# An attention block with fused feed-forward: loads for the last stage two blocks sooner, and another interleaving of eight steps on TensorE

## Chip, cores and metric

One core of a Trainium2 chip. The metric is the device time of one execution in microseconds. Three runs of the kernel before gave 2847.31, 2848.78 and 2850.04 us.

## The reference

Two residual layers on `x` of shape (4, 2048, 256), all in fp32, 16 heads of 16 channels:

```python
x = x + attention(layernorm(x), Wq, bq, Wk, bk, Wv, bv, Wo, bo)   # logits = q k^T * 4, softmax over 2048 keys
y = layernorm(x)
y_prev = y shifted by one token (zero ahead of the first)
xr, xk = mu_r * y + (1 - mu_r) * y_prev, mu_k * y + (1 - mu_k) * y_prev
out = x + sigmoid(xr @ W_r) * (square(relu(xk @ W_k)) @ W_v)
```

The softmax subtracts each query's largest logit, so for each query and head the maximum over all 2048 keys has to be known before its exponentials.

## The kernel before, in words

Two stages lie in one program: `stage_attend` (layer norm, projections, attention) and `stage_mix` (output projection, second norm, feed-forward). Constants and buffers of the second stage live in `MixInputs`, called `ahead` in the first, because parts of it start early.

**Attention.** Work is cut into 64 blocks (`ITS`), each of 512 queries for four heads; a block has 16 steps (`CH`), each of 128 keys. For a step:
- Two fills (`scores`, L1130 ff.) put logits into PSUM, each for two heads: two f16 matmuls (L1136) side by side on two halves of the rows of the array, 512 columns each. PSUM has two pairs of banks for them, so `fill(n)` waits until ACT is through with fill n - 2 (`s_exp`).
- ACT takes the exponential of each pair of banks (L921, 128x1024) into one of three `p_sb` buffers (in the profile `m_gate`, `m_y` and `p_x`).
- `times_v` (L1217 ff., matmul at L1233) multiplies by V with a column of ones: four column groups of the array, fp32. It runs whole (512 columns) or in two halves (256 columns each, `times_v(n, 0)` and `times_v(n, 1)`); in the first step of a block the first half is always whole and the second does nothing. It waits for both exponentials of its step.

**The maxima** of a later block are found meanwhile. A pack (`peaks`, L1172 ff., matmul at L1192) makes the logits of 128 queries of two heads against 512 keys in two of three banks, again two f16 matmuls; the pack waits until the first bank of the pack before has been reduced (`s_mx`). DVE reduces each bank to a column of `mx` (L998). Some packs are "larger": ahead of them two key ranges are subtracted (`differences`, L1151, a fill of its own that ACT copies through a ReLU into `copied`, L930), and DVE adds and reduces in one custom operation with an accumulator read (L993), so that one pack stands for two. `LARGER` says which packs of a period these are, `COPY_AT` at which fills the copies stand, `EXPS_BEFORE` before which exps ACT runs them.

**Order.** Eight steps are a period (`SPAN`), two periods a block. In a period PE runs 16 fills for exps, 2 fills for copies, 14 packs and 8 `times_v`, in an order written out by hand in `tensor` (L1348 to L1397). Maxima run three periods (`LEAD`) ahead of the fills; the loop has 125 periods, and the rest follows with `last_fills`, into which `early` mixes parts of the second stage. In every second period `turn` (L1195 ff.) transposes the block's maxima; its place among the fills is `TURN_AT`. They come from `of_block` on DVE (L977) and `chain` on POOL (L803 ff.); ACT copies the result to `a_mrows` (L897), and SP sends it into the rows of the next block's queries (`rows`, L699), for which the first fill of that block waits (`s_mr`). Because all engines follow written orders, the unit numbers of fills, copies and turns come from the constants at the head (L488 to L506).

**The way into the last stage.** SP runs `body(it)` per block and ahead of some bodies, at L768 to L790, loads for the second stage. They hang together: `load_sums` brings the denominators of a sequence, DVE inverts them (`invert`, L1109), `store_inverse` writes them out (SP waits for it), `load_heads` brings numerators and inverses, and POOL multiplies them (`heads`, L858, in the trace L317) for the output projection, which `early` starts on PE. In the kernel before POOL runs `heads` of blocks 0 and 1 ahead of the last `chain`.

Of the kernel before, what the change touches and what calls it, by code (L numbers as in the profile page):

```python
# [32 lines left out]
ITS = UNITS * QB  # L33
# [440 lines left out]
def stage_attend(ctx, nc, psum, x, wqT, wkT, wvT, bq, bk, q_d, k_d, kd_d, v_d, sums_d, inputs, ahead):  # L474
# [16 lines left out]
    FULL, LESS = 16, 14  # L491
    LARGER = (4, 7)
    COPY_AT = (0, 11)
    EXPS_BEFORE = (0, 10)
    COPIES = 2 * (PERIODS - LEAD)
# [6 lines left out]
    CHAIN = 5  # L502
    FILLS_AHEAD = 3
    TURN_AT = 14
    FIRST_LEAD = QB + 2
# [165 lines left out]
    def sync(sp):  # L671
# [95 lines left out]
        for it in range(ITS):  # L767
            if it == ITS - 4:  # L768
                ahead.load_constants(sp)
                for seq in range(B - 1):  # L770
                    ahead.load_sums(sp, seq)
            if it == ITS - 2:
                ahead.store_inverse(sp, 0)
                sp.wait_ge(ahead.s_rden[0], DMA)
                for n in range(2):
                    ahead.load_heads(sp, n)
                for n in range(2):
                    ahead.load_x(sp, n)
                for n in range(2, 4):
                    ahead.load_heads(sp, n)  # L780
# [12 lines left out]
    def gpsimd(pool):  # L793
# [61 lines left out]
        for pit in range(1, ITS):  # L855
            if pit % QB == 0:
                copy_v(pit // QB, range(CH // 2))
            if pit == ITS - 1:  # L858
                for n in range(2):
                    ahead.heads(pool, n)  # L860
            chain(pit)
            if pit % QB == 0:
                copy_v(pit // QB, range(CH // 2, CH))
# [108 lines left out]
    def vector(dve):  # L972
# [132 lines left out]
        for n in range(FULL * LEAD, PACKS):  # L1105
            if n == first_pack(PERIODS - 2):
                ahead.spread_bias(dve)
# [22 lines left out]
    def tensor(te):  # L1130
# [195 lines left out]
        for blk in range(BLOCKS):  # L1326
# [15 lines left out]
            lead(blk, 4)  # L1342
        av.wait(te, BLOCKS - 1, "v1")
        for n in range(3):
            fill(n)
        for n in range(0):
            peaks(FULL * LEAD + n)
        for p in range(PERIODS - LEAD):  # L1348
            f, n, c = FILLS * p, FULL * LEAD + LESS * p, SPAN * p
            fill(f + 3)  # L1350
            fill(f + 4)
            peaks(n)
            times_v(c)
            peaks(n + 1)
            fill(f + 5)
            times_v(c + 1, 0)
            peaks(n + 2)
            fill(f + 6)
            fill(f + 7)
            times_v(c + 1, 1)  # L1360
            peaks(n + 3)
            fill(f + 8)
            times_v(c + 2, 0)
            peaks(n + 4)
            fill(f + 9)
            times_v(c + 2, 1)
            fill(f + 10)
            peaks(n + 5)
            times_v(c + 3, 0)
            fill(f + 11)  # L1370
            peaks(n + 6)
            fill(f + 12)
            times_v(c + 3, 1)
            fill(f + 13)
            peaks(n + 7)
            times_v(c + 4)
            peaks(n + 8)
            if p % 2 and p + 1 < PERIODS:
                turn((p + 1) // 2)
            fill(f + 14)  # L1380
            times_v(c + 5, 0)
            peaks(n + 9)
            fill(f + 15)
            times_v(c + 5, 1)
            fill(f + 16)
            peaks(n + 10)
            fill(f + 17)
            times_v(c + 6, 0)
            peaks(n + 11)
            fill(f + 18)  # L1390
            times_v(c + 6, 1)
            fill(f + 19)
            peaks(n + 12)
            times_v(c + 7, 0)
            fill(f + 20)
            peaks(n + 13)
            times_v(c + 7, 1)  # L1397
        for n in range(SPAN * (PERIODS - LEAD), STEPS):
# [298 lines left out]
```

## Time and profile before

| | us |
|---|---|
| profiled execution | 2846.68 |
| its span, first to last instruction | 2844.8 |
| PE busy (modelled ends) | 2783.0 |
| DVE busy | 2528.2 |
| ACT busy | 2516.7 |
| POOL busy | 377.9 |

The projections take the first 230 us, the attention loop runs from there to about 2540, and the last stage ends the program. In a timeline a row is a start, a length, an engine, a line, an operation with its tiles and a count; `x8` of L1233 is one visit of `times_v`. Records of consecutive operations may overlap, so the distance of starts says more than the length.

### The profile page before, as it was taken

Reading aid. Unit: us, or ns where it says so; the run is one execution under the profiler, and the core shown is the slowest. Engines: PE = TensorE matmul, PEld = TensorE weight load, DVE = VectorE, ACT = ScalarE, POOL = GpSimd, SP = SyncE. Lnnn points to the kernel's source line nnn. Section 1 sums busy time; section 2 is a strip of 40 time slices with the busy share of each in tenths; the row PEclk is TensorE's granted clock in tenths of the full one; section 3 lists DMA queues with packets and bytes.
Section 4 is the critical chain, followed back from the end, with each engine's and each line's share of the span. In section 5 each row is a group of like instructions: output and inputs, shape, how many; then the busy total and the mean of one; then the engine's idle time right before and its main releaser. Section 6 shows DMA issues by size and latency. Waiting matters only on the chain.

```text
span 2844.8 us, 60963 instructions
## 1 busy us (share of the span) xinstructions
PE 2783.0 (98%) x24132; PEld 907.4 (32%) x24132; DVE 2528.2 (89%) x4794; ACT 2516.7 (88%) x2874; POOL 377.9 (13%) x752
## 2 busy tenths in 40 slices
PE   8999999999999999999999999999999999999998
PEld 4543222222222222222222222222222222224776
DVE  4567999999999999999999999999999999975773
ACT  6768999999999999999999999999999999986555
POOL 6762000000000000000000000000000000013541
PEclk9999999999999999999999999999999999999999
DMA  5642000000000000000010101010101000123431
GB/s 172 198 152 74 18 20 20 22 22 22 22 22 22 22 22 22 22 17 26 11 31 8 32 11 32 11 33 11 33 11 32 11 28 15 31 79 98 161 108 45
DMA packets 135276, 124.41 MB, mean 44 GB/s; under 512 B 49872, under 2 KB 117328, under 8 KB 134992
## 3 DMA queue, kind: packets, MB, share of 16 engines
q1 hardware_dynamic: 134992, 120.52, 13.7%
q8 instruction: 191, 3.13, 0.4%
q14 instruction: 93, 0.76, 0.1%
HBM read 72.75 MB, written 47.19 MB: 42 GB/s over the span
## 4 chain that ended last, share of the span: by engine, by line
PE 73%; ACT 16%; issue 5%; DVE 4%; DMA 1%; SPq 0%; POOLq 0%; POOL 0%; ACTq 0%; DVEq 0%
PE psum L1233 30%; PE psum L1136 16%; PE psum L1192 14%; ACT m_gate L921 4%; ACT p_x L921 4%; ACT m_y L921 4%; PE psum L1256 3%; PE psum L1569 2%; PE psum L443 2%; PE psum L1151 2%; PE psum L1267 1%; ACT a_copied L930 1%; PE psum L1590 1%; DVE m_split L413 1%; DMA a_qs<-a_mrows 1%
## 5 line engine op out<-in xcount | busy, mean ns | idle before, releaser
L998 DVE TENSOR_REDUCE a_mx<-psum 128x1 f32<-128x512 f32 x3096 | 1958.3, 684 | 134.3 <-PE psum L1192 92.5
L1136 PE MATMUL psum<-a_qs,a_ks 50*128 50x512 f16 x4096 | 774.6, 385 | 12.2 <-DMA a_qs<-a_mrows 7.5
L921 ACT ACTIVATE m_gate<-psum 128x1024 f32<-128x1024 f32 x684 | 674.9, 1029 | 44.7 <-PE psum L1136 39.3
L921 ACT ACTIVATE p_x<-psum 128x1024 f32<-128x1024 f32 x682 | 673.0, 1029 | 41.1 <-PE psum L1136 35.6
L921 ACT ACTIVATE m_y<-psum 128x1024 f32<-128x1024 f32 x682 | 673.0, 1029 | 36.9 <-PE psum L1136 31.3
L1192 PE MATMUL psum<-a_ks,a_qs 48*128 48x512 f16 x3596 | 696.5, 384 | 4.5 <-DVE a_mx L998 4.1
L1233 PE MATMUL psum<-m_gate,a_vst 128*32 128x256 f32 (+1 forms) x4736 | 418.4, 425 | 4.0 <-ACT m_gate L921 0.9
L1233 PE MATMUL psum<-p_x,a_vst 128*32 128x256 f32 (+1 forms) x4728 | 417.6, 425 | 3.1
L1233 PE MATMUL psum<-m_y,a_vst 128*32 128x256 f32 (+1 forms) x4728 | 417.3, 425 | 3.0
L1136 PEld LDWEIGHTS psum<-a_qs,a_ks 50*128 50x128 f16 x4096 | 197.6, 93 | 546.4 <-issue 140.5
L1192 PEld LDWEIGHTS psum<-a_ks,a_qs 48*128 48x128 f16 x3596 | 175.1, 93 | 556.2 <-DVE a_mx L998 435.6
L993 DVE CUSTOM_DVE_ANT_0 a_copied<-psum,a_copied 128x512 f32<-128x512 f32 x500 | 325.0, 688 | 18.3 <-PE psum L1192 1.9
L930 ACT ACTIVATE a_copied<-psum 128x1024 f32<-128x1024 f32 x250 | 256.8, 1027 | 0.5 <-PE psum L1151 0.5
L807 POOL MEMSET a_mx<- 128x8 f32 x64 | 7.2, 113 | 1455.8 <-DVE a_m L977 1455.8
L1233 PEld LDWEIGHTS psum<-m_gate,a_vst 128*32 128x32 f32 x4736 | 93.7, 108 | 201.6 <-issue 164.7
L1233 PEld LDWEIGHTS psum<-p_x,a_vst 128*32 128x32 f32 x4728 | 93.7, 108 | 200.3 <-issue 165.8
L1233 PEld LDWEIGHTS psum<-m_y,a_vst 128*32 128x32 f32 x4728 | 93.7, 108 | 199.8 <-issue 166.5
L800 POOL COPY a_vst<-a_vin 128x64 f32<-128x64 f32 x256 | 60.1, 238 | 694.9 <-PE psum L1233 694.9
L1151 PE MATMUL psum<-a_kd,a_qs 48*128 48x512 f16 x500 | 96.2, 381 | 0.4 <-ACT m_v L886 0.4
L822 POOL TENSOR_TENSOR m_split<-m_whole,m_split 128x512 f16<-128x512 f32 x64 | 73.7, 1157 | 72.1 <-ACT m_split L909 71.8
L907 ACT ACTIVATE m_whole<-psum,p_sb,p_gain 128x512 f32<-128x512 f32 x64 | 49.5, 773 | 27.7 <-PE psum L1256 27.7
L363 DVE TENSOR_TENSOR m_whole<-psum,m_x 128x512 f32<-128x512 f32 x24 | 16.4, 689 | 58.8 <-PE psum L443 51.2
(120 smaller groups left out, 1641.5 us busy)
## 6 DMA issues: line engine op xcount, KB each, us to landing
m_x<-x SPq DMA_DIRECT2D x24, 512.0 KB, 5.1
a_qs<-q_parts SPq DMA_DIRECT2D x384, 32.0 KB, 2.1
sums<-a_o SPq DMA_DIRECT2D x256, 34.0 KB
q_parts<-m_split SPq DMA_DIRECT2D x16, 512.0 KB, 3.2
v_rows<-m_v SPq DMA_DIRECT2D x16, 512.0 KB, 2.7
k_parts<-m_split SPq DMA_DIRECT2D x16, 512.0 KB, 3.9
a_ks<-k_parts SPq DMA_DIRECT2D x64, 128.0 KB
a_vin<-v_rows SPq DMA_DIRECT2D x64, 128.0 KB, 5.5
```

The source lines that it names most:

```text
L443: mm = te.matmul(bank[:, (t % 2) * C:(t % 2 + 1) * C], self.hT[blk % 2][:, k, t * P:(t + 1) * P], self.w_sb["o"][:, k, :], start=(k == 0), ...
L800: pool.tensor_copy(v_st[:, c, :, 0:D], v_in[:, u % 2, c, :].rearrange("p (g d) -> p g d", g=G)).then_inc(s_vc, 1)
L822: least.done(pool.tensor_tensor(parts[s][:, j, 1, :], full[s][:, j, :], parts[s][:, j, 0, :], ALU.subtract))
L921: ac.activation(p_sb[n % WEIGHTS][:, 2 * pair:2 * pair + 2, :], psum[:, at:at + 2, :], ACT.Exp, scale=SCALE).then_inc(s_exp, 1)
L930: ac.activation(copied[:, :, :], psum[:, at:at + 2, :], ACT.Relu).then_inc(s_exp, 1)
L993: dve.tensor_tensor_reduce(out=copied[:, par, :], in0=psum[:, bank(at), :], in1=copied[:, par, :], scale=1.0, scalar=LEAST, op0=ALU.add, o ...
L998: dve.tensor_reduce(peak, psum[:, bank(at), :], AX.X, ALU.max).then_inc(s_mx, 1)
L1136: mm = te.matmul(psum[:, pair_of_banks(u) + par, :], ks[row:row + MR, (it // QB) % 2, pair, c * P:(c + 1) * P], qs[row:row + MR, it % QRIN ...
L1151: mm = te.matmul(psum[:, pair_of_banks(u) + par, :], qs[row:row + SR, pit % QRING, at:at + P], kd[row:row + SR, (pit // QB) % 2, pair, :], ...
L1192: te.matmul(psum[:, bank(slot(n, par)), :], qs[row:row + SR, pit % QRING, at:at + P], keys, start=True, stop=True).then_inc(s_sp, 1)
L1233: mm = te.matmul(psum[32 * g:32 * g + 32, O, at:at + width], v_st[:, c, g, :], p_sb[n % WEIGHTS][:, g, at:at + width], start=(c == 0), sto ...
L1256: mm = te.matmul(psum[:, j % 2, :], w_sb[n][:, k, h * P:(h + 1) * P], xnT[blk % 2][:, k, :], start=(k == 0), stop=(k == KH - 1))
```

## The change

Steps move and constants change; no operation is added or left out.
- `FILLS_AHEAD` 3 to 4: four fills stand ahead of the loop instead of three, and three packs as well (before: none), so the loop body runs `fill(f + 4)` to `fill(f + 21)` and `peaks(n + 3)` to `peaks(n + 16)`.
- Copies at fills 1 and 13 instead of 0 and 11, larger packs 3 and 13 instead of 4 and 7.
- The turn at fill 7 instead of 14.
- Whole `times_v` for steps c + 1 and c + 7; before, c and c + 4.
- SP, POOL and DVE: loads and their partners two blocks (DVE: four periods) sooner; `heads` behind `chain` of block 61 instead of ahead of that of block 63.

```diff
-    LARGER = (4, 7)
-    COPY_AT = (0, 11)
-    EXPS_BEFORE = (0, 10)
+    LARGER = (3, 13)
+    COPY_AT = (1, 13)
+    EXPS_BEFORE = (1, 12)
-    FILLS_AHEAD = 3
-    TURN_AT = 14
+    FILLS_AHEAD = 4
+    TURN_AT = 7
@@ sync
-            if it == ITS - 4:
+            if it == ITS - 6:
                 ahead.load_constants(sp)
                 for seq in range(B - 1):
                     ahead.load_sums(sp, seq)
-            if it == ITS - 2:
+            if it == ITS - 4:
                 ahead.store_inverse(sp, 0)
                 sp.wait_ge(ahead.s_rden[0], DMA)
                 for n in range(2):
                     ahead.load_heads(sp, n)
                 for n in range(2):
                     ahead.load_x(sp, n)
+            if it == ITS - 3:
                 for n in range(2, 4):
                     ahead.load_heads(sp, n)
@@ gpsimd
-            if pit == ITS - 1:
+            chain(pit)
+            if pit == ITS - 3:
                 for n in range(2):
                     ahead.heads(pool, n)
-            chain(pit)
@@ vector
-            if n == first_pack(PERIODS - 2):
+            if n == first_pack(PERIODS - 6):
@@ tensor, ahead of the loop
+        for n in range(4):
+            fill(n)
         for n in range(3):
-            fill(n)
-        for n in range(0):
             peaks(FULL * LEAD + n)
```

The loop body after the change, whole:

```python
            fill(f + 4)
            times_v(c, 0)
            peaks(n + 3)
            fill(f + 5)
            times_v(c, 1)
            fill(f + 6)
            peaks(n + 4)
            times_v(c + 1)
            if p % 2 and p + 1 < PERIODS:
                turn((p + 1) // 2)
            peaks(n + 5)
            fill(f + 7)
            times_v(c + 2, 0)
            fill(f + 8)
            peaks(n + 6)
            times_v(c + 2, 1)
            fill(f + 9)
            peaks(n + 7)
            fill(f + 10)
            times_v(c + 3, 0)
            peaks(n + 8)
            fill(f + 11)
            times_v(c + 3, 1)
            fill(f + 12)
            peaks(n + 9)
            times_v(c + 4, 0)
            fill(f + 13)
            peaks(n + 10)
            fill(f + 14)
            times_v(c + 4, 1)
            peaks(n + 11)
            fill(f + 15)
            times_v(c + 5, 0)
            fill(f + 16)
            peaks(n + 12)
            times_v(c + 5, 1)
            fill(f + 17)
            peaks(n + 13)
            fill(f + 18)
            times_v(c + 6, 0)
            peaks(n + 14)
            fill(f + 19)
            times_v(c + 6, 1)
            fill(f + 20)
            peaks(n + 15)
            times_v(c + 7)
            fill(f + 21)
            peaks(n + 16)
```

## Rows read from the trace of the kernel before

**Rows 1.** The page: busy time of each engine, its share, instructions.

```profile
PE 2783.0 (98%) x24132; PEld 907.4 (32%) x24132; DVE 2528.2 (89%) x4794; ACT 2516.7 (88%) x2874; POOL 377.9 (13%) x752
```

**Rows 2.** Windows view, then the turns by line, 526 to 2474 us.

```profile
526.00:2474.00 1948.00, 1935.15 (x18713) 510.36 (x18712) 1882.89 (x3448) 1847.87 (x2014) 91.35 (x424) 1.00 0.08 22
...
L1200 PE MATMUL psum<-a_ident,a_mparts x54: 229/230/230, 525.9 to 2473.8; 128*32 128x128 f16 x54
```

**Rows 3.** Timeline of PE: start, length, line, out<-in, count.

```profile
1487.96 0.73 PE L1136 MATMUL psum<-a_qs,a_ks 50*128 50x512 f16 x4
1488.52 0.38 PE L1192 MATMUL psum<-a_ks,a_qs 48*128 48x512 f16 x2
1488.86 1.06 PE L1233 MATMUL psum<-m_y,a_vst 128*32 128x512 f32 x8
1489.86 0.39 PE L1192 MATMUL psum<-a_ks,a_qs 48*128 48x512 f16 x2
1490.09 0.38 PE L1136 MATMUL psum<-a_qs,a_ks 50*128 50x512 f16 x2
1490.62 0.64 PE L1233 MATMUL psum<-p_x,a_vst 128*32 128x256 f32 x8
1491.19 0.39 PE L1192 MATMUL psum<-a_ks,a_qs 48*128 48x512 f16 x2
1491.41 0.63 PE L1136 MATMUL psum<-a_qs,a_ks 50*128 50x512 f16 x4
...
1492.54 0.39 PE L1192 MATMUL psum<-a_ks,a_qs 48*128 48x512 f16 x2
1492.92 0.39 PE L1136 MATMUL psum<-a_qs,a_ks 50*128 50x512 f16 x2
1493.24 0.64 PE L1233 MATMUL psum<-m_gate,a_vst 128*32 128x256 f32 x8
...
1497.76 0.38 PE L1192 MATMUL psum<-a_ks,a_qs 48*128 48x512 f16 x2
...
1500.24 0.39 PE L1192 MATMUL psum<-a_ks,a_qs 48*128 48x512 f16 x2
```

**Rows 4.** Timeline of ACT, same stretch.

```profile
1487.22 1.02 ACT L921 ACTIVATE m_y<-psum 128x1024 f32<-128x1024 f32 x1
...
1488.61 1.96 ACT L921 ACTIVATE p_x<-psum 128x1024 f32<-128x1024 f32 x2
...
1491.84 1.02 ACT L921 ACTIVATE m_gate<-psum 128x1024 f32<-128x1024 f32 x1 [0.24 <-PE psum L1136]
```

**Rows 5.** Timeline of DVE, around a larger pack.

```profile
1498.18 0.69 DVE L993 CUSTOM_DVE_ANT_0 a_copied<-psum,a_copied 128x512 f32<-128x512 f32 x1
1498.79 0.08 DVE L993 DVE_READ_ACCUMULATOR2_ANT a_mx<- 128x1 f32 x1
...
1499.49 1.89 DVE L998 TENSOR_REDUCE a_mx<-psum 128x1 f32<-128x512 f32 x3
```

**Rows 6.** Timeline of DVE and POOL, from the block's maxima to the turn.

```profile
1507.91 0.21 DVE L977 TENSOR_REDUCE a_m<-a_mx 128x16 f32<-128x64 f32 x1
...
1508.98 0.22 POOL L816 TENSOR_TENSOR a_mparts<-a_m,a_mparts 128x16 f16<-128x16 f32 x1
```

**Rows 7.** Timeline of POOL, ahead of the last turn.

```profile
2539.30 2.50 POOL L317 TENSOR_TENSOR m_hT<-m_num,m_rden 128x512 f32<-128x512 f32 x2 [35.47 <-DMA m_rden<-inverse_denominators]
```

**Rows 8.** DVE's reduces by line, 100 to 262 us: ns min/median/max.

```profile
L998 DVE TENSOR_REDUCE a_mx<-psum x123: 673/681/693, 100.6 to 261.4; 128x1 f32<-128x512 f32 x123
```

**Rows 9.** Timeline of PE at the end of attention, then the windows view.

```profile
2562.16 0.39 PE L1136 MATMUL psum<-a_qs,a_ks 50*128 50x512 f16 x2 [3.65 <-DMA a_qs<-a_mrows]
...
2564.73 1.78 PE L1233 MATMUL psum<-p_x,a_vst 128*32 128x512 f32 x8
...
2562.00:2566.00 4.00, 3.84 (x16) 1.35 (x16) 0.00 (x0) 2.05 (x2) 0.00 (x0) 0.60 0.00 0
```

**Rows 10.** Timeline of PE, first `times_v` of the loop.

```profile
237.20 1.93 PE L1233 MATMUL psum<-m_gate,a_vst 128*32 128x512 f32 x8
```

More of the change, by code:

```diff
@@ L1349, in tensor @@
             f, n, c = FILLS * p, FULL * LEAD + LESS * p, SPAN * p
-            fill(f + 3)
             fill(f + 4)
-            peaks(n)
-            times_v(c)
-            peaks(n + 1)
+            times_v(c, 0)
+            peaks(n + 3)
             fill(f + 5)
-            times_v(c + 1, 0)
-            peaks(n + 2)
+            times_v(c, 1)
             fill(f + 6)
[L1359 to L1363, printed above, removed]
@@ L1364, in tensor @@
-            peaks(n + 4)
[L1365 to L1377, printed above, removed]
+            peaks(n + 4)
+            times_v(c + 1)
             if p % 2 and p + 1 < PERIODS:
                 turn((p + 1) // 2)
+            peaks(n + 5)
@@ L1380, in tensor @@
+            fill(f + 7)
+            times_v(c + 2, 0)
+            fill(f + 8)
+            peaks(n + 6)
+            times_v(c + 2, 1)
+            fill(f + 9)
+            peaks(n + 7)
+            fill(f + 10)
+            times_v(c + 3, 0)
+            peaks(n + 8)
+            fill(f + 11)
+            times_v(c + 3, 1)
+            fill(f + 12)
+            peaks(n + 9)
+            times_v(c + 4, 0)
+            fill(f + 13)
+            peaks(n + 10)
             fill(f + 14)
+            times_v(c + 4, 1)
@@ L1381, in tensor @@
+            peaks(n + 11)
+            fill(f + 15)
             times_v(c + 5, 0)
-            peaks(n + 9)
-            fill(f + 15)
+            fill(f + 16)
+            peaks(n + 12)
             times_v(c + 5, 1)
-            fill(f + 16)
-            peaks(n + 10)
             fill(f + 17)
+            peaks(n + 13)
+            fill(f + 18)
             times_v(c + 6, 0)
-            peaks(n + 11)
-            fill(f + 18)
+            peaks(n + 14)
+            fill(f + 19)
             times_v(c + 6, 1)
-            fill(f + 19)
@@ L1393, in tensor @@
-            peaks(n + 12)
-            times_v(c + 7, 0)
             fill(f + 20)
-            peaks(n + 13)
-            times_v(c + 7, 1)
+            peaks(n + 15)
+            times_v(c + 7)
+            fill(f + 21)
+            peaks(n + 16)
         for n in range(SPAN * (PERIODS - LEAD), STEPS):
```

## Prediction

> **What bounds the kernel now.** The engines' busy line comes first: PE 98%, DVE 89%, ACT 88% [rows 1]. PE's share is of modelled ends, so it hides short waits; I read start to start instead. From 526 to 2474 us the kernel repeats one block (one `it`, two periods) and PE, DVE and ACT are all busy there for 95 to 99% of the stretch; 54 turns of the maxima lie 1947.9 us apart, so a block takes 1947.9 / 53 = 36.75 us [rows 2]. The 125 periods of the main loop are 62.5 blocks, some 2300 of the 2844.8 us. So 0.1 us in a block is worth 6 us.
>
> PE's own time of a block follows from start-to-start distances where nothing is waited for [rows 3]: a half `times_v` to what follows 0.57 (1490.62 to 1491.19), a whole one 1.00 (1488.86 to 1489.86), a fill or a pack to the next f16 pair 0.23 (1489.86 to 1490.09), to a `times_v` 0.31 (1492.92 to 1493.24); the turn adds about 0.48 in place of 0.31 (estimate, one per block). Counting the loop body: 24 halves and 4 wholes (17.7), of the 64 f16 pairs 28 stand before a `times_v` (8.7) and 35 before another pair (7.9), and the turn: 34.8. The other 2.0 us of 36.75 are waits. They are of three kinds:
> - A pack (`peaks`) may start 0.06 us after DVE's first reduce of the pack before it ended: 1499.49 + 0.68, then 1500.24 [rows 3, 5, 8]. DVE starts 0.42 after PE does (1497.76 to 1498.18) and needs 2 x 0.61 a pack (one larger pack: 1498.18 to 1499.49, 1.31) [rows 3, 5]. So a pack follows the last at the soonest after 0.42 + 0.69 + 0.06 = 1.16, and in a run of packs after 1.21; if it comes more than some 0.06 later, DVE idles. PE and DVE have almost no play.
> - A fill may start 0.05 after the exp of the fill two before it: 1487.22 + 1.02, and the second of the two fills at 1487.96 starts at 1488.52 - 0.23 = 1488.29. ACT starts 0.43 after an awaited fill (1491.41, 1491.84), and takes an exp each 0.91 to 0.94 (1488.61 + 1.96 holds two of 1.02, overlapped) [rows 3, 4].
> - A `times_v` waits 0.05 after both exps of its step: 1488.61 + 1.96, then 1490.62, where PE was free at 1490.09 + 0.31 = 1490.40 [rows 3, 4].
>
> **The loop body, counted.** After the change a block has 22 halves and 5 wholes (step c+1 and c+7 in both periods; step c is one call with all columns only where a block begins): 27 visits, not 28. PE's own time by the same prices is 34.45, so -0.32. Then the ledger from pack to pack. Before: 11 gaps of 1.11, 12 of 1.33, 4 of 1.31, one of 1.36. Short and long ones alternate, so each 1.11 is lifted only to 1.16 (three times to 1.19, behind a larger pack or the reduce of a block's maxima): +0.6, 35.4. After: 13 of 1.11, 9 of 1.33, 3 of 1.53, one each of 1.31, 1.47 and 0.68. The 0.68 (`peaks(n + 3)`, two fills, `peaks(n + 4)`, in the period where step c is whole) is lifted to 1.16 (+0.48); of the 1.11 seven are lifted to 1.16 (+0.34), and six that follow another short gap to 1.21 (+0.64): 34.45 + 1.46 = 35.9. Against DVE alone the new order is thus 0.5 us worse.
>
> But before stands at 36.75, not 35.4: 1.35 us more, and these are waits for ACT. I see them at the two fills 0.23 apart at 1487.96, at `times_v(c + 1, 0)` (0.22), at `fill(f + 8)` (1492.54 + 0.23 = 1492.77, started at 1492.92 [rows 3]); by the same rules `fill(f + 17)` waits 0.2, and the second period repeats all but the first. Their cause is two adjacent fills (two pairs in a period) and exps needed some 2.1 us after their fill. A fill that had to wait has its exp two exps later, 0.91 + 1.02 + 0.05, so that `times_v` has to be 2 us or more behind. After: four fills ahead; one adjacent pair in a block instead of four; the lead from a step's last fill to its `times_v` is 2.3 to 3.0 in six steps of eight and 1.9 and 2.1 in two (before: 1.6 to 2.1 in five of eight). I walked one block of the new order by hand with the three rules. Waits for ACT remain at `fill(f + 6)` (0.38, inside the 0.68 gap, where DVE makes PE wait anyway), and of 0.05 to 0.1 at `fill(f + 14)`, `fill(f + 18)` in gaps that are short as well. The walk ends at 36.0. The same walk over before's first period gives 18.37, half of 36.74, against the 36.75 measured.
>
> One size is open: how soon a pack may follow the first reduce of a larger pack. In before each larger pack stands ahead of a long gap and never holds PE. The nearest row has the custom operation ending 0.69 after its start like a plain reduce, so 0.06 behind it; the other bound is that PE is held until the next reduce could have been read, some 0.14 more (an estimate: the record of that reduce, 1498.18, is followed by an accumulator read of 0.08, and the packs behind in before come 0.2 behind its end and don't wait) [rows 5]. After the change larger packs 3 and 13 both stand ahead of short gaps: with the dearer value the walk ends at 36.4. I take 36.13, nearer to the lower end, as the record itself says. 36.75 - 36.13 = 0.62, times 62.5: **-39 us** (ends -22 and -47).
>
> What the rules make of drain: a half costs 0.57, the two 256-column halves 1.14 and 0.31 - 0.23 more for the second entry, a whole 1.00 [rows 3]. The Trainium skill ("TensorEngine Tiling (Array Packing)", Key Properties) says that a change of tiling mode drains TensorE, and the trace agrees, with 0.57 x 2 + 0.08 - 1.00 = 0.22 us for the second visit. By that rule alone, waits left as they are, the change would bring one visit less, 0.32 x 62.5 = 20 us; that is the case "waits kept" below.
>
> **The turn, seven fills sooner.** It waits for the block reduce on DVE and four POOL operations: 1507.91 to 1508.98 + 0.22, 1.3 us [rows 6]. In the new body the pack behind which that reduce runs starts some 6.6 us of PE time ahead of the turn: no wait. Behind the turn on PE all is queued, behind `keep_rows` on ACT one exp; ACT has slack there. The rows' transfer gets 10 us of PE time until `fill` of the next block, against 4.6 before. In the steady blocks that was nearly enough.
>
> **Loads two blocks sooner.** SP: constants and three sums at `ITS - 6`, the inverse, heads and x at `ITS - 4`, heads 2 and 3 at `ITS - 3`. The wait of SP for the stored inverse now holds back the queries of block 63 and the rows of block 61; both are needed over 20 us later. POOL runs the two `heads` behind `chain(61)`; before, POOL sat 35.47 us in front of them, with `chain(63)` behind [rows 7]. They cost 2 x 2.50 us of POOL, which is idle for most of a block. DVE's bias, shares and inverse move by four periods at the same cost. In the steady stretch DVE reads PSUM while POOL would work: in the lead stage, with POOL at `m_split`, 123 reduces took 673 to 693 ns [rows 8]. The Trainium skill ("SBUF — State Buffer", Who interferes with whom) has GpSimd and DVE lock each other out only for some forms and never for `tensor_reduce` on this chip; by it the moved heads cost nothing, and if they did hold DVE it would be the 5 us once.
>
> What this buys is at the end: the last turn, seven fills sooner, with its chain no longer behind `heads`. Before, PE waited 3.65 us for the last rows, and then the granted clock was 0.60 in that stretch (part of it at 1.2 GHz): the eight L1233 took 1.78 instead of 1.06, and the four L443 in front of them were as slow [rows 9, 3]. 3.65 + 0.7 + 0.7 (an estimate for L443, by the same stretch) = 5.0. Next late there is DVE's first normalisation, which hangs on the same PE work and moves with it: **-5 us**.
>
> **The start.** Three packs now stand in front of the loop, each DVE-bound with nothing between them: fill 4 comes some 2 us later, while PE is at half clock (L1233 1.93 [rows 10]). In return the last period has three packs less. Between 0 and +4; **+2 us**.
>
> Sum: -39 - 5 + 2 = -42. The profiled execution took 2846.68 (span 2844.8), the median is 2848.78; the same difference from the median gives **2807**.
>
> **Rivals.**
> - Waits kept: PE saves its visit, the 2.0 us of waits stay: -20 - 5 + 2: 2826. For it: the three engines are within 5% of each other, waits move rather than vanish. Chance 0.17.
> - Slower: the lock of PE with DVE. If the ACT waits fall outside the short gaps, they add to the ledger as they do before: 35.9 + 1.35 = 37.25, with dearer larger packs 37.6: +0.5 to +0.85 a block, +28 to +50 with the ends: 2877 to 2899. It decides where ACT waits outside short gaps exceed 36.75 - 35.9 = 0.85 a block. For it: DVE's record shows idle time before a larger pack already; against: leads of exps grow everywhere. Chance 0.12.
> - A wash: ACT waits of 0.8 to 0.95 a block outside the gaps: 2843 to 2854. Chance 0.08; that the packing changes nothing because the rows or the clock decide is in it.
> - More: the fills no longer wait, packs behind larger ones cost nothing, PE near its ledger without the 0.48: 35.5 a block, -78: under 2785. Chance 0.05.
> - The forecast's case, 36.0 to 36.4: 2799 to 2824, likeliest 2807. Chance 0.58.
>
> 8 in 10: 2790 to 2852, over the forecast, "waits kept" and most of the wash. About 0.2% (5.7 us) is what a measurement can tell. Faster 0.79, same 0.07, slower 0.14.
>
> **What would show it.** The distance of 54 turns over 53 near 36.1; L1233 x8 of 512 columns in 5 of 27 visits; no idle time of `fill(f + 8)` and `times_v(c + 1)` behind ACT, but PE waiting at `peaks(n + 4)` and DVE idle in front of larger pack 3; no wait for `a_mrows` at the end. Wrong if blocks take 36.7 or more: then the ACT waits have moved to long gaps, or the larger packs hold PE.

## Result, and the profile after

| | before | after |
|---|---|---|
| median of 4 runs, us | 2848.05 | 2807.39 |
| lowest to highest | 2842.58 to 2850.04 | 2806.26 to 2811.90 |
| profiled execution (span) | 2846.68 (2844.8) | 2811.90 (2810.0) |
| granted clock over the span | 0.997 | 0.995 |

The ratio after to before is 0.9867, with an interval of 0.9855 to 0.9879: 41 us faster, and the median lies 0.4 us from the predicted 2807. That the total fits does not say that its terms do: between the two profiled executions the spans differ by 34.8 us, where my terms add up to 42. So the fit to 0.4 us is luck; the rest of the text goes by terms. The matmuls fall from 24132 to 23628, by 504, eight for each visit of `times_v` saved: two half visits became one whole. Lines of the kernel after stand one higher than before: L1137 is the fill, L1193 the pack, L1234 `times_v`, L1201 the turn, L922 the exp.

**The loop.** The answer to [rows 1], from the page of the kernel after (busy us, share, instructions):

```profile
PE 2746.6 (98%) x23628; PEld 927.1 (33%) x23628; DVE 2494.8 (89%) x4794; ACT 2493.5 (89%) x2874; POOL 375.9 (13%) x752
```

The answers to [rows 2], windows view and turns by line of the kernel after (for the turns: ns least/median/most, first and last start):

```profile
520.00:2445.00 1925.00, 1906.37 (x18325) 525.68 (x18323) 1863.06 (x3458) 1832.39 (x2019) 94.54 (x428) 1.00 0.08 24
...
L1201 PE MATMUL psum<-a_ident,a_mparts x53: 218/219/220, 553.0 to 2438.0; 128*32 128x128 f16 x53
```

1885.0 us for 52 blocks is 36.25, but one of them, from 2362.34 to 2401.85, takes 39.51: DVE's one-time work for the last stage lies in it, and PE waits for DVE in front of one pack (1.64). The granted clock is 0.5 right behind that wait, so that the block costs 3.3 us more than its neighbours and not 1.8 (PE's timeline; 1.06 would be due):

```profile
2395.43 1.93 PE L1234 MATMUL psum<-m_gate,a_vst 128*32 128x512 f32 x8
```

Before, it lay between 2473.81 and 2513.55, outside the stretch that I had read, with a wait of 1.57 at 2502.68, half clock soon after, and 3.1 us in sum. It moved and nearly kept its price. The other 51 blocks take (1885.0 - 39.5) / 51 = 36.19; before, 36.75.

The page shows nothing of this: PE 98% and DVE 89% both times, ACT 88% and 89%. What moved is in the distances. This is the second period of a block and its turn in the kernel after (timeline of PE; start, length, line, out<-in, count), to be held against [rows 3]:

```profile
1485.87 0.39 PE L1193 MATMUL psum<-a_ks,a_qs 48*128 48x512 f16 x2
...
1486.47 0.64 PE L1234 MATMUL psum<-m_y,a_vst 128*32 128x256 f32 x8
1487.17 0.39 PE L1193 MATMUL psum<-a_ks,a_qs 48*128 48x512 f16 x2
...
1488.86 1.06 PE L1234 MATMUL psum<-p_x,a_vst 128*32 128x512 f32 x8
1489.86 0.39 PE L1137 MATMUL psum<-a_qs,a_ks 50*128 50x512 f16 x2
1490.09 0.38 PE L1193 MATMUL psum<-a_ks,a_qs 48*128 48x512 f16 x2
1490.31 0.38 PE L1137 MATMUL psum<-a_qs,a_ks 50*128 50x512 f16 x2
1490.62 0.64 PE L1234 MATMUL psum<-m_gate,a_vst 128*32 128x256 f32 x8
...
1492.90 1.06 PE L1234 MATMUL psum<-m_y,a_vst 128*32 128x512 f32 x8
1493.78 0.22 PE L1201 MATMUL psum<-a_ident,a_mparts 128*32 128x128 f16 x1
1493.93 0.39 PE L1193 MATMUL psum<-a_ks,a_qs 48*128 48x512 f16 x2
```

A fill, a pack and a fill follow each other 0.23 and 0.22 apart (1489.86, 1490.09, 1490.31), and `times_v` comes 0.31 behind: no wait among four operations. The whole `times_v` at 1492.90 is followed by the turn after 0.88 and by a pack 0.15 later. The pack at 1487.17 stands 0.70 behind a half instead of 0.57; that is the pack behind a larger one (1485.87). DVE and ACT in the same stretch ([rows 4 to 6]):

```profile
1486.33 0.68 DVE L994 CUSTOM_DVE_ANT_0 a_copied<-psum,a_copied 128x512 f32<-128x512 f32 x1
1486.94 0.08 DVE L994 DVE_READ_ACCUMULATOR2_ANT a_mx<- 128x1 f32 x1
...
1490.50 1.29 DVE L999 TENSOR_REDUCE a_mx<-psum 128x1 f32<-128x512 f32 x2 [0.25 <-PE psum L1193]
...
1490.36 1.94 ACT L922 ACTIVATE m_y<-psum 128x1024 f32<-128x1024 f32 x2 [0.55 <-PE psum L1137]
```

The custom reduce of the larger pack starts at 1486.33 and the next pack at 1487.17, 0.84 later; by the rule for plain packs it would be 0.68 + 0.06 = 0.74. So this larger pack holds the next by 0.10, between my ends 0 and 0.14. It is the only one of a block's four that does: behind pack 13 of the other period the next pack waits 0.01. DVE and ACT both stand idle for a moment here (0.25 and 0.55, ended by PE): neither holds PE at this place.

By position in the loop body, own time of PE and waits come out as follows, in us of a block: means of the start-to-start distances at each position over all blocks, the costs of [rows 3] taken off, what is left counted as a wait. (The 0.95 holds 0.06 of the one long block.)

| | before | after |
|---|---|---|
| PE's own time | 34.77 | 34.33 |
| waits in front of fills | 1.19 | 0.79 |
| in front of packs | 0.37 | 0.95 |
| in front of `times_v` | 0.43 | 0.20 |
| mean block | 36.75 | 36.25 |
| undisturbed block (median) | 36.67 | 36.17 |

**The rows' transfer.** Before, some blocks were longer than 36.67, up to 38.02, and together these excesses come to 5.7 us. Of these, 4.2 us in six blocks stand at the block's first fill, which waits for the rows; the other 1.5 us stand at other places. The longest block runs from 1701.46 to 1739.48, and PE's timeline of before has the cause in it:

```profile
1707.59 0.39 PE L1136 MATMUL psum<-a_qs,a_ks 50*128 50x512 f16 x2 [1.28 <-DMA a_qs<-a_mrows]
```

The idle times by releaser name that transfer at nine fills before, between 526 and 2500 us (6.6 us in front of their weight loads). After, they name it once in the whole run, with 1.1 us in front of the weight load at 2449.25, and up to there the excesses come to 0.9. That one wait comes from the moved loads. SP's timeline after has the rows' transfer of block 61 in the last line:

```profile
2431.71 10.94 SPq L153 DMA_DIRECT2D a_qs<-q_parts  x6
2442.70 2.71 SPq L699 DMA_DIRECT2D a_qs<-a_mrows  x4
```

The turn of that block is at 2437.98, so SP issues the transfer 4.72 behind it, where other blocks have 0.57. Ahead of it stand, in SP's written order, a wait of 6.8 us for the stored inverse, the loads of heads and x from 2425.05 on, and the queries, whose six issues take 10.94 us here and 3.61 in the block before. The block takes 36.95, 0.8 more than its neighbours. In the kernel with the order alone (below), where those loads aren't at this place, the queries' issues take 2.86, the rows' transfer starts 0.56 behind its turn, and the fill isn't late.

**The end.** The answers to [rows 7, 9], timelines of POOL and PE after:

```profile
2444.07 2.50 POOL L317 TENSOR_TENSOR m_hT<-m_num,m_rden 128x512 f32<-128x512 f32 x2 [6.21 <-DMA m_rden<-inverse_denominators]
...
2511.43 0.22 PE L1201 MATMUL psum<-a_ident,a_mparts 128*32 128x128 f16 x1
...
2549.72 2.08 PE L443 MATMUL psum<-m_wo,m_hT 128*128 128x256 f32 x4 [2.34 <-DVE m_xT L431]
...
2552.27 1.93 PE L1234 MATMUL psum<-p_x,a_vst 128*32 128x512 f32 x8
...
2554.68 1.50 PE L443 MATMUL psum<-m_wo,m_hT 128*128 128x256 f32 x3
```

The wait of 3.65 for the last rows is gone, and POOL has multiplied the heads 65 us before the last turn. The wait for DVE at 2549.72 is not new; new is what stands behind it. Before, the same wait, of 2.37 us, was followed by full speed, in the timeline of PE of the kernel before:

```profile
2588.26 1.13 PE L443 MATMUL psum<-m_wo,m_hT 128*128 128x256 f32 x4 [2.37 <-DVE m_xT L431]
...
2590.97 1.13 PE L443 MATMUL psum<-m_wo,m_hT 128*128 128x256 f32 x4
```

The windows view has the granted clock as the third number from the right; behind the wait it is 1.00 in the kernel before,

```profile
2588.00:2592.00 4.00, 3.73 (x20) 1.70 (x20) 3.96 (x10) 1.89 (x2) 0.00 (x0) 1.00 0.43 164
```

and 0.50 in the kernel after:

```profile
2550.00:2554.00 4.00, 4.00 (x14) 1.21 (x14) 3.96 (x10) 1.02 (x1) 0.00 (x0) 0.50 0.32 122
```

From one L443 to the next it is 2.71 before and 4.96 after (2549.72 to 2554.68): 2.25 us go back to the clock, at 1.2 instead of 2.4 GHz.

**The start.** The answer to [rows 10], PE after; the first operation of the loop's fills is at 234.73, before at 232.90:

```profile
238.55 0.61 PE L1193 MATMUL psum<-a_ks,a_qs 48*128 48x512 f16 x2 [0.78 <-DVE a_mx L999]
239.94 0.61 PE L1193 MATMUL psum<-a_ks,a_qs 48*128 48x512 f16 x2 [0.78 <-DVE a_mx L999]
...
240.90 1.93 PE L1234 MATMUL psum<-m_gate,a_vst 128*32 128x512 f32 x8
```

From first fill to first `times_v` it is 6.17 against 4.30: two of the three packs wait 0.78 each for DVE.

**All of it.** The span's difference of -34.8 us between the two profiled executions is +1.8 up to the first fill (the stage ahead, which the change doesn't touch), +1.9 to the first `times_v`, -36.9 to the bias matmul (L340), -2.5 to the last stage, +0.9 in the last stage. The medians differ by 40.7; the profiled execution of after lies 4.5 above its median, that of before 1.4 below.

### The profile page after: what moved, and what is told of

Read it like the earlier page. It is cut to its first block, busy times and chain, and to the rows that moved or that the text cites. A ratio compares the mean times of both kernels' runs of the same rounds, so it can differ in the third digit from the quotient of the medians.

```text
span 2810.0 us, 59956 instructions
## 1 busy us (share of the span) xinstructions
PE 2746.6 (98%) x23628; PEld 927.1 (33%) x23628; DVE 2494.8 (89%) x4794; ACT 2493.5 (89%) x2874; POOL 375.9 (13%) x752
## 4 chain that ended last, share of the span: by engine, by line
PE 78%; SPq 9%; ACT 5%; DVE 4%; issue 2%; DMA 2%; POOLq 0%; POOL 0%; ACTq 0%; DVEq 0%
PE psum L1234 33%; PE psum L1137 17%; PE psum L1193 15%; PE psum L1257 3%; SPq L153 3%; SPq L158 2%; PE psum L1152 2%; PE psum L1570 2%; PE psum L443 2%; SPq L126 2%; SPq L127 2%; PE psum L1268 2%; DMA a_qs<-q_parts 2%; PE psum L1591 1%; ACT m_gate L922 1%
## 5 line engine op out<-in xcount | busy, mean ns | idle before, releaser
L999 DVE TENSOR_REDUCE a_mx<-psum 128x1 f32<-128x512 f32 x3096 | 1948.8, 685 | 122.4 <-PE psum L1193 101.8
L1137 PE MATMUL psum<-a_qs,a_ks 50*128 50x512 f16 x4096 | 794.1, 384 | 12.6 <-ACT m_gate L922 1.7
L922 ACT ACTIVATE m_gate<-psum 128x1024 f32<-128x1024 f32 x684 | 674.7, 1034 | 41.3 <-PE psum L1137 38.4
L1193 PE MATMUL psum<-a_ks,a_qs 48*128 48x512 f16 x3596 | 696.7, 384 | 13.7 <-DVE a_mx L999 5.5
L922 ACT ACTIVATE p_x<-psum 128x1024 f32<-128x1024 f32 x682 | 672.9, 1034 | 41.5 <-PE psum L1137 38.9
L922 ACT ACTIVATE m_y<-psum 128x1024 f32<-128x1024 f32 x682 | 672.8, 1034 | 40.3 <-PE psum L1137 37.6
L1234 PE MATMUL psum<-m_gate,a_vst 128*32 128x256 f32 (+1 forms) x4568 | 414.8, 435 | 1.6 <-ACT m_gate L922 0.9
L1234 PE MATMUL psum<-p_x,a_vst 128*32 128x256 f32 (+1 forms) x4568 | 412.9, 433 | 0.8
L1234 PE MATMUL psum<-m_y,a_vst 128*32 128x256 f32 (+1 forms) x4552 | 412.0, 434 | 0.8
L1137 PEld LDWEIGHTS psum<-a_qs,a_ks 50*128 50x128 f16 x4096 | 199.3, 93 | 611.1 <-issue 135.0
L1193 PEld LDWEIGHTS psum<-a_ks,a_qs 48*128 48x128 f16 x3596 | 175.3, 93 | 463.3 <-DVE a_mx L999 368.1
L1234 PEld LDWEIGHTS psum<-m_gate,a_vst 128*32 128x32 f32 x4568 | 90.7, 108 | 191.4 <-issue 174.9
L1234 PEld LDWEIGHTS psum<-p_x,a_vst 128*32 128x32 f32 x4568 | 90.8, 108 | 189.8 <-issue 175.0
L1234 PEld LDWEIGHTS psum<-m_y,a_vst 128*32 128x32 f32 x4552 | 90.4, 108 | 189.8 <-issue 174.5
```

The lines of the kernel that those rows point to most:

```text
L922: ac.activation(p_sb[n % WEIGHTS][:, 2 * pair:2 * pair + 2, :], psum[:, at:at + 2, :], ACT.Exp, scale=SCALE).then_inc(s_exp, 1)
L999: dve.tensor_reduce(peak, psum[:, bank(at), :], AX.X, ALU.max).then_inc(s_mx, 1)
L1137: mm = te.matmul(psum[:, pair_of_banks(u) + par, :], ks[row:row + MR, (it // QB) % 2, pair, c * P:(c + 1) * P], qs[row:row + MR, it % QRIN ...
L1193: te.matmul(psum[:, bank(slot(n, par)), :], qs[row:row + SR, pit % QRING, at:at + P], keys, start=True, stop=True).then_inc(s_sp, 1)
L1234: mm = te.matmul(psum[32 * g:32 * g + 32, O, at:at + width], v_st[:, c, g, :], p_sb[n % WEIGHTS][:, g, at:at + width], start=(c == 0), sto ...
```

## Experiments

Times are medians of four runs (ten for the loads alone); the ratio is to runs of the kernel before taken beside them, with a 95% interval. "Block" is the median distance of two turns.

### The order alone

Before with the new order, the constants of fills, copies and larger packs, and the old places of all loads.

```diff
-            if it == ITS - 6:
+            if it == ITS - 4:
                 ahead.load_constants(sp)
...
+            if pit == ITS - 1:
+                for n in range(2):
+                    ahead.heads(pool, n)
             chain(pit)
-            if pit == ITS - 3:
-                for n in range(2):
-                    ahead.heads(pool, n)
...
-            if n == first_pack(PERIODS - 6):
+            if n == first_pack(PERIODS - 2):
```

> The changed kernel with the loads for the last stage, POOL's heads, and DVE's bias and inverse back where they were. My theory: the main loop alone gives the gain (36.17 us a block as in the changed kernel), and only the end suffers: the last chain on POOL stands behind heads again, which waited for the inverses until 2539 us in the kernel before, so the last turn, now due seven fills sooner, makes PE wait some 4 to 9 us. About 2812 to 2820. Rival (the loads matter by themselves, by keeping transfers out of the end): 2830 or more.

Measured: 2818.91, ratio 0.9907 (0.9892 to 0.9922). A block takes 36.17 as in after, and the loop from the first `times_v` to the bias matmul 2264.5 us (after: 2265.6). So the whole gain of the loop is the order's. The kernel takes 11.5 us more than after by the medians; between the two profiled executions the stretch behind the bias matmul is 7.7 us longer. PE's timeline, then POOL's:

```profile
2509.75 1.13 PE L443 MATMUL psum<-m_wo,m_hT 128*128 128x256 f32 x4 [1.74 <-POOL m_hT L317]
...
2511.13 1.92 PE L1233 MATMUL psum<-p_x,a_vst 128*32 128x512 f32 x8
2517.49 0.29 PE L1200 MATMUL psum<-a_ident,a_mparts 128*32 128x128 f16 x1 [4.44 <-POOL a_mparts L816]
...
2513.99 2.48 POOL L317 TENSOR_TENSOR m_hT<-m_num,m_rden 128x512 f32<-128x512 f32 x2 [4.30 <-DMA m_rden<-inverse_denominators]
2516.42 0.11 POOL L807 MEMSET a_mx<- 128x8 f32 x1
```

The turn, seven fills sooner, meets a chain that POOL can't begin until the second `heads` is done, and that one waits for its transfer.

### The loads alone

```diff
-            if it == ITS - 4:
+            if it == ITS - 6:
                 ahead.load_constants(sp)
```

and the other hunks of SP, POOL and DVE in the same way, on the kernel before.

> The kernel before with only the loads, heads, bias and inverse moved two blocks sooner. My theory: the loop stays at 36.67 us a block; the last chain is no longer behind heads, but the turn stays at fill 14, so PE's wait for the last rows stays or shrinks by the 6.7 us transfer having less beside it (3.65 down to 0): 2842 to 2849. Rival (the loads bring the gain): under 2830.

Measured: 2842.68, ratio 0.9988 (0.9978 to 0.9997), against 2845.62 for before. An undisturbed block takes 36.67, as before. The profiled execution is the highest of the ten (2849.63) and holds a few longer blocks, so it can't show a small cost or the lack of one. In the kernel after, the reduces beside POOL's `heads` (L999, 2430 to 2450 us) take 680 to 693 ns as elsewhere, the answer to [rows 8]: POOL's `heads` don't slow them. The loads alone are worth some 3 us (1 to 6 by the interval) and with the order 11.5: they are what lets the early turn stand at the end.

### The turn back at fill 14

The kernel after, with the turn ahead of `fill(f + 14)`.

```diff
-    TURN_AT = 7
+    TURN_AT = 14
...
             times_v(c + 1)
-            if p % 2 and p + 1 < PERIODS:
-                turn((p + 1) // 2)
             peaks(n + 5)
...
             peaks(n + 10)
+            if p % 2 and p + 1 < PERIODS:
+                turn((p + 1) // 2)
             fill(f + 14)
```

> The changed kernel with the turn back at fill 14. My theory: the rows' transfer gets 4.6 us of PE time again; some blocks wait for it (5 to 6 us over the loop, as the irregular intervals of 37 and 38 us did before) and the last rows make PE wait up to 3.6 us and run some us at the lower clock: 2815 to 2822. Rival (the place of the turn is only a matter of PE order, the transfer hides anyway): within 2 us of the changed kernel, 2805 to 2810.

Measured: 2869.66, ratio 1.0084 (1.0069 to 1.0099). I had it at 2815 to 2822: a miss of some 50 us. A block takes 37.12. PE's timeline at the turn:

```profile
1496.07 0.39 PE L1152 MATMUL psum<-a_kd,a_qs 48*128 48x512 f16 x2
...
1496.79 0.22 PE L1201 MATMUL psum<-a_ident,a_mparts 128*32 128x128 f16 x1
1497.61 0.39 PE L1137 MATMUL psum<-a_qs,a_ks 50*128 50x512 f16 x2 [0.61 <-ACT a_copied L931]
```

The turn's result goes into one of the two pairs of banks of the fills. Copy fill 13, turn and fill 14 follow each other within 0.9 us here (1496.07 to 1496.79 + 0.16), so fill 14 waits until ACT has copied fill 13. With that (0.67 a block), the turn's own place (0.11) and the rows' transfer, which is now waited for in nearly every block (53 times between 500 and 2500 us, 21.6 us in front of weight loads; 0.28 a block at the first fill), it makes 1.06; other waits shrink by 0.1, and a block loses 0.95. The early turn is thus worth 62 us in this order; I had given it 8 to 15.

### Three fills ahead in the new order

```diff
-    FILLS_AHEAD = 4
-    TURN_AT = 7
+    FILLS_AHEAD = 3
+    TURN_AT = 6
...
-            fill(f + 4)
+            fill(f + 3)
```

and so on for every fill of the body; the copies, too, come one place later on PE.

> The changed kernel with the same sequence of kinds on PE, but three fills ahead instead of four: every fill of the loop is the one before (and the turn at fill 6, so that it stands at the same place). PE's own time of a block stays 34.45 us and so does the ledger of packs. My theory (exps needed too soon after their fills made the waits of the kernel before): leads of times_v shrink by about one fill, 0.9 us, to 0.9 to 2.1 us, under the 2.2 that two queued exps need, in most steps; waits of 0.2 to 0.8 us in many of them, 0.5 to 2 us a block: 2840 to 2930. Rival (fewer visits and the smoother packs make the gain, the lead does not matter): 2807 to 2812.

Measured: 3163.40, ratio 1.1118 (1.1101 to 1.1135), far above the 2840 to 2930 expected. PE's timeline:

```profile
1502.85 0.38 PE L1137 MATMUL psum<-a_qs,a_ks 50*128 50x512 f16 x2
1504.35 0.64 PE L1234 MATMUL psum<-p_x,a_vst 128*32 128x256 f32 x8 [1.12 <-ACT p_x L922]
```

and one of three such lines of idle times by releaser, 500 to 2500 us (us in total, times, longest):

```profile
PEld psum L1234 <- ACT p_x L922: 157.6, 160, 1.7
```

A `times_v` needs the exp of a fill that started 0.3 us ahead of it where nothing waits; with 0.42 until ACT starts, 1.02 for the exp and 0.05 it is 1.50 behind that fill (1502.85 to 1504.35). A block takes 41.8. That the fourth fill ahead is a needed part of this order held; its size, 5.7 us a block, I had missed (356 us over after, where my upper end had 123), having walked only single waits and not their sum over eight steps.

### The visit alone

On the kernel before, `times_v(c + 7)` whole: two visits fewer in a block.

```diff
-            times_v(c + 7, 0)
+            times_v(c + 7)
...
-            times_v(c + 7, 1)
```

> The kernel before with one edit: step c + 7 whole, in the place of its first half. Two visits of times_v less in a block, so PE's own time falls by 0.6 us a block. The rule of counting visits: -0.6 x 62.5 = -38 us, 2810. My theory (packs are locked to DVE): the pack gaps 1.33 and 1.33 become 1.54 and 0.68, and the 0.68 is held to 1.16 by DVE: 2.70 instead of 2.67, so nothing of the 0.6 is kept, and three fills within 0.7 us wait for ACT inside that: 2845 to 2870.

Measured: 2898.09, ratio 1.0175 (1.0158 to 1.0192), 28 us above the upper end of what I expected. PE's own time falls from 34.77 to 34.31, as counting says, and yet a block grows to 37.53. PE's timeline:

```profile
1518.00 0.39 PE L1136 MATMUL psum<-a_qs,a_ks 50*128 50x512 f16 x2
...
1518.45 0.38 PE L1136 MATMUL psum<-a_qs,a_ks 50*128 50x512 f16 x2
1519.51 0.39 PE L1136 MATMUL psum<-a_qs,a_ks 50*128 50x512 f16 x2 [0.69 <-ACT m_y L921]
```

Three fills stand at 1518.00, 1518.45 and 1519.51; the third could have started at 1518.67 and waits 0.84 for the exp of the first, twice in a block. I had named DVE as what holds PE; it is ACT. The Trainium skill ("TensorEngine Tiling (Array Packing)", Key Properties) says that a change of tiling mode drains TensorE. The trace agrees in PE's own time, 0.46 us less for two visits; the kernel's time doesn't follow it. So a count of visits is no forecast: by it this kernel would have come to some 2810.

### The first larger pack two packs later

```diff
-    LARGER = (3, 13)
+    LARGER = (5, 13)
```

> The changed kernel with the first larger pack of each period at 5 instead of 3, so that it stands ahead of a gap of 1.33 us instead of the 0.68 one (even periods). By the ledger the 0.68 gap is then held to 1.16 instead of some 1.25, and pack 5's 1.31 fits its gap: -0.1 to -0.2 us a block, 2795 to 2802. Rival (the place of a larger pack does not matter, DVE's total is the same): within 2 us of 2807.

Measured: 2806.21, ratio 0.9857 (0.9842 to 0.9872), a block 36.16: no difference from after, where I expected 5 to 12 us less; the rival holds. The 0.19 that a block waits at pack 4 stays, though pack 3 is now a plain one. So it isn't the larger pack that holds it.

### The short gap taken out

The kernel after; in the periods where step c is whole, step c + 1 in halves, the first ahead of `fill(f + 6)`.

```diff
+            if p % 2 == 0:
+                times_v(c + 1, 0)
             fill(f + 6)
             peaks(n + 4)
-            times_v(c + 1)
-            if p % 2 and p + 1 < PERIODS:
-                turn((p + 1) // 2)
-            peaks(n + 5)
-            fill(f + 7)
+            if p % 2 == 0:
+                times_v(c + 1, 1)
+                fill(f + 7)
+                peaks(n + 5)
+            else:
+                times_v(c + 1)
+                if p + 1 < PERIODS:
+                    turn((p + 1) // 2)
+                peaks(n + 5)
+                fill(f + 7)
```

> The changed kernel, with step c + 1 in two halves in the periods where a block begins: fill 5, first half, fill 6, pack 4, second half, fill 7, pack 5. PE's own time rises by 0.31 us a block, but the gap of 0.68 between packs 3 and 4, which with its waits (fill 6 for ACT 0.30, pack 4 for DVE 0.20) took 1.18, becomes 1.33, and packs 3 to 6 take 1.33 + 1.16 + 1.21 = 3.70 instead of 1.18 + 1.31 + 1.33 = 3.82. My theory: -0.12 us a block, 2798 to 2803. Rival (every visit of times_v costs its 0.31): +0.31 a block, 2825.

Measured: 2814.31, ratio 0.9888 (0.9871 to 0.9904), 11 us above what I expected; a block takes 36.26 instead of 36.17. After has here (PE's timeline):

```profile
1509.69 0.39 PE L1193 MATMUL psum<-a_ks,a_qs 48*128 48x512 f16 x2
1509.92 0.92 PE L1137 MATMUL psum<-a_qs,a_ks 50*128 50x512 f16 x4
1510.87 0.39 PE L1193 MATMUL psum<-a_ks,a_qs 48*128 48x512 f16 x2
```

and the experiment:

```profile
1511.75 0.39 PE L1193 MATMUL psum<-a_ks,a_qs 48*128 48x512 f16 x2
1511.97 0.38 PE L1137 MATMUL psum<-a_qs,a_ks 50*128 50x512 f16 x2
1512.50 0.64 PE L1234 MATMUL psum<-m_gate,a_vst 128*32 128x256 f32 x8
...
1513.30 0.38 PE L1193 MATMUL psum<-a_ks,a_qs 48*128 48x512 f16 x2
```

In after two packs stand 1.18 apart with 0.68 of work between them, so 0.50 of waits; in the experiment they stand 1.55 apart. The waits of the gap went as expected, but the visit costs 0.22, the first half of step c + 1 now stands only 1.95 behind the last fill of its exps and waits 0.22 (1511.97 + 0.31 = 1512.28, started 1512.50), and packs 5 to 8 behind it wait 0.06 to 0.09 each (in after only 7 and 8). The short gap of the new order is the cheaper choice, by 0.09 us a block.

### The fourth fill alone, in the old order

```diff
-    FILLS_AHEAD = 3
-    TURN_AT = 14
+    FILLS_AHEAD = 4
+    TURN_AT = 15
...
-            fill(f + 3)
             fill(f + 4)
+            fill(f + 5)
```

and so on for every fill of the body.

> The kernel before with the same sequence of kinds on PE, but four fills ahead instead of three: every fill of the loop is the next one (the turn at 15, at its old place; copies stay at 0 and 11 of the period and so come one place sooner). My theory: waits of times_v (0.22 and 0.07 us a block before step c + 1) vanish, waits of fills for ACT (1.2 us a block) stay, since they depend on how the fills are spaced and not on which they are: 36.3 to 36.6 us a block; the first fill of a block is also one place nearer to its turn, so waits for the maxima's rows may take 0.1 to 0.3 back. 2828 to 2848. Rival (the fourth fill ahead is the gain, the order only follows): 36.2 a block or less, under 2822.

Measured: 2988.24, ratio 1.0495 (1.0480 to 1.0511): 142 us slower than before, where I had no more than 2848. PE's timeline, then ACT's:

```profile
1523.87 0.39 PE L1136 MATMUL psum<-a_qs,a_ks 50*128 50x512 f16 x2
1525.57 0.39 PE L1136 MATMUL psum<-a_qs,a_ks 50*128 50x512 f16 x2 [1.31 <-ACT m_y L921]
...
1524.01 0.59 ACT L935 COPY a_o<-psum 128x512 f32<-128x512 f32 x1 [0.88 <-PE psum L1233]
1524.49 1.95 ACT L921 ACTIVATE m_y<-psum 128x1024 f32<-128x1024 f32 x2
```

ACT follows its written order, in which the exp of 1524.49 stands behind the copy. It comes to the output copy of the block (L935) before PE has done the block's last `times_v`, stands 0.88 in front of it with a filled pair of banks behind, and the fill that needs these banks starts 1.47 late. The rest of the loss is smaller waits at other fills, and the rows' transfer, which comes later to each block by one fill (waited for in front of fills 49 times, 16.4 us).

### The output copy one exp pair later

On the kernel of the last experiment.

```diff
-                if c == 0 and it:
-                    keep_output(it - 1)
+                    if (c, pair) == (1, 0) and it:
+                        keep_output(it - 1)
```

> The kernel with four fills ahead in the old order (lead_only, 2988 us), with one edit on ACT: the copy of a finished block's output stands behind the exp of one more fill. Theory formed on the last run: there ACT stood 0.88 us in front of that copy, waiting for the last times_v of the block, with an exp that was ready queued behind it, and the fill two further on waited 1.47 us on PE. With the copy one exp later ACT's wait goes, the fill's 1.47 falls to 0.1 to 0.5, and times_v of the new block, which needs the bank the copy reads, waits some 0.3 to 0.9 instead: 0.5 to 1 us a block less, 2925 to 2960. Rival (the loss of the fourth fill in the old order comes from the spacing of fills and the later rows): no change, 2980 or more.

Measured: 2905.45, ratio 1.0205 (1.0188 to 1.0222), 83 us less than without the edit. Time of ACT in front of L935 goes from 56.5 us (63 times) to 1.2, and the fill waits 0.17 instead of 1.47. So the place of the copy is shown to be the cause of 83 of the 142 us; the other 58 are the smaller waits and the rows' transfer (17.1 us in front of 48 fills), which no run takes apart. The edit returned more than expected, since the first `times_v` of the next block, which I had waiting for the later copy, waits only 0.03. In the kernel after, the block's last step stands whole ahead of `fill(f + 21)`, and the idle time of ACT in front of the copy is 0.9 us in all the stretch from 500 to 2440 (in the kernel before there is none): the new order avoids by its sequence what the fourth fill brings into the old one.

## Why the prediction held, point by point

- **PE's own time of a block:** predicted 34.8 and 34.45, measured 34.77 and 34.33. The prices of single distances carry over to another order; the 0.12 are the turn, which starts 0.88 behind a whole `times_v` where 1.00 would be due. Of the 0.44 by which the own time falls, about half is the visit (0.22) and half the turn, which now stands behind a whole `times_v` and no longer between two f16 pairs.
- **A block:** predicted 36.13 with the ends 36.0 and 36.4, measured 36.17 (mean 36.19) against 36.67 (mean 36.75). Waits after: predicted 1.46 for DVE and some 0.2 for ACT, in sum 1.7; measured 1.9, and the own time is 0.12 less. Two misses cancel here, and the fit of the block is in part luck. The check of the walk on before was so too: its 36.74 met a mean of 36.75 that held longer blocks, where the undisturbed block, which it had walked, takes 36.67. In single places: `fill(f + 6)` 0.30 and `peaks(n + 4)` 0.20, where I had 0.38 for the fill and 0.48 for the gap that holds both; `fill(f + 14)` 0.12 in both periods, `fill(f + 18)` 0.05 and 0.14 (0.05 to 0.1 predicted). Not predicted: 0.11 of the first `times_v` of a block, 0.15 behind the end of the output copy, for which it waits. The 0.13 at `peaks(n + 14)` in one period is the pack behind the larger one, below. Two signs that I had named are there: PE waits at `peaks(n + 4)`, and DVE stands idle for 0.35 in front of larger pack 3 (at 1510.11); no fill f + 8 and no `times_v(c + 1)` waits for ACT.
- **The kind of the waits:** half right. I said that the waits of before for ACT go and DVE's lock with PE takes their place. In front of packs it is 0.95 instead of 0.37, in front of `times_v` 0.20 instead of 0.43; but in front of fills 0.79 remain of 1.19. So the sum of the waits has hardly moved, 1.99 to 1.94: as the rival "waits kept" has it, the gain is in PE's own time (0.44, with the turn more than its 0.32), and the order is what keeps the waits from growing as visits go. Merging halves in the old order (two visits less) lets them grow from 1.99 to 3.28. Which of the other moves in the order does it (the copies, the three packs ahead, the choice of whole steps) no run takes apart; two are shown to be needed, the fourth fill and the early turn. My account of a block had the right rules and sizes, but its telling, waits for ACT gone, is not what the sum shows: the step that failed is the fall of the waits from 2.0 to 1.7.
- **The larger pack:** 0.10 of a range of 0 to 0.14, at one of four. The rival that its place costs nothing further was right; moving it from pack 3 to 5 changed nothing.
- **The loop's term:** predicted -39, measured 2302.5 - 2265.6 = -36.9 between first `times_v` and bias matmul. Of this 62.5 x 0.50 = 31 is the undisturbed block and 3.4 are the waits for the rows' transfer (4.2 us before, 0.8 after). Here the working was loose. I took the block of before with its irregular ones (36.75), and wrote that the rows' transfer "was nearly enough" in the steady blocks: it was most of the difference from 36.67. So the -39 held part of a gain whose cause I had set at nothing. Some 2 us of the term I can't place.
- **The start:** +2 predicted, +1.9 measured. The stage ahead ended 1.8 later in this profile; the change doesn't touch it.
- **The end:** -5 predicted, -2.5 measured from bias matmul to last stage (67.9 to 65.4). The 3.65 wait and its half clock went; the step that failed is "next late there is DVE's first normalisation, which ... moves with it": it moved with it, but the wait of 2.34 was followed by half clock, which gave 2.25 back.
- **The loads at no cost:** nearly right. DVE's reduces aren't slowed. But the rows of block 61, which I had "needed over 20 us later", are needed 11.3 us behind their turn (2437.98 to 2449.25); SP sends them 4.2 us late, and that costs 0.8 us once in this execution. The size varies: 0.3 in the run with the short gap taken out, none in the run with the larger pack moved. What I hadn't said is that the early turn needs the loads: without them 11.5 us are lost.
- **The early turn:** I argued that it doesn't wait and helps the end. In the loop it is worth far more, because late in this order it would stand between two uses of the fills' banks. Since I predicted the change as made and not the part alone, the total didn't suffer; the sizes that I gave to parts in the experiments did (the turn at fill 14, three fills ahead, and the fourth fill alone were each off by over 40 us). The parts don't add up: against before, the fourth fill alone costs 142 us, all but the fourth fill 318, all but the early turn 24.

## What to carry to other kernels

Where three engines are within a few per cent of each other, price single operations by the distance of their starts, then walk the written order with the two or three rules of who waits for whom; a count of operations or visits can point the wrong way. Look for what stands still in order on an engine (an output copy, a transpose that borrows a buffer) before running another queue further ahead: the wait in front of it holds all that is behind. Judge such a reordering as a whole, for its parts alone can each be slower than what they replace.

## What the chip showed that I had not expected

- The granted clock after a short wait of PE differs between kernels with the same wait. Behind 2.37 us before it is 1.00 and L443 takes 1.13; behind 2.34 us after it is 0.50, and L443 takes 2.08 and L1234 1.93. Behind the wait of 1.64 us for DVE's one-time work it is 0.5 in the kernel after (`times_v` 1.93), and the block is 3.3 us over its neighbours; in the run with the larger pack moved the same 1.64 us are followed by 1.00 (`times_v` 1.06), and the block is 1.8 us over. In the kernel with the order alone, a wait of 1.74 in front of L443 at 2509.75 is followed by a L443 of 1.13 and a L1233 of 1.92. So such a wait carries a risk of some 2 us beyond its length, and no run here says when.
- A larger pack's custom reduce with accumulator read frees its bank 0.10 later for PE than a plain reduce (0.84 from start to next pack, against 0.74).
